# A gated cross-attention and mixture-of-experts layer: expert 0's low weight parts on VectorE, and Silu for the experts' gate

## Chip, core and metric

The kernel runs on one core of a Trainium2 chip. The metric is the device time of one execution in microseconds (us), lower is better. Profile times are us from the start of the span unless ns is written. TensorE does the matmuls (PE in the profile, its weight loads PEld), VectorE is DVE, ScalarE is ACT, GpSimd is POOL, and SyncE (SP) issues most of the transfers.

## What is computed

x is 8 batches of 256 tokens by 512. First a cross attention without softmax is added to x: the score is the sigmoid of a product over the 256 positions, scaled by 1/16. Then a mixture of 16 experts, top 4 per token, is added.

```python
x = x + tanh(g_xattn[0]) * xattn(layernorm(x), ctx, ctx)      # score = sigmoid(Q^T K / 16); out = V score
t = rmsnorm(layernorm(x)) * norm_w
logits = t @ gate_w.T + gate_b
vals, idx = top_k(logits, 4);  gates = softmax(vals)          # scattered to G[token, expert]
h = einsum('mh,eoh->emo', t, w1) + b1
a = minimum(h[..., ::2], 7.0)
b = clip(h[..., 1::2], -7.0, 7.0)
act = a * sigmoid(1.702 * a) * (b + 1.0)
y = einsum('emi,edi->emd', act, w2) + b2
x = x + tanh(g_ffn[0]) * einsum('me,emd->md', G, y)
```

## The kernel before

**Split products.** The large matmuls take their fp32 operands in two parts: a rounded high part (ScalarE writes it, `W1h`, `W2h`, `xTh`, `hTh`, `Kh`, `Qh`), and the low part, which is the value less the high part (`W1l`, `W2l`, `xTl`, `hTl`, `Kl`, `Ql`). Each product is three passes: high by high, low by high, high by low.

**Attention stage** (0 to some 145 us). The engines each run an own list, written out by hand, over the batches b = 0 to 7. TensorE: products of K and Q (`qk`, L397), of scores and V (`av`, L409), turning of the normed tokens of batch b-1 (L417), their logits (L426), and the rank of the tokens within an expert (`rank`, L437). ScalarE: sigmoid of the scores, the scale of the tokens (`scale_t`, L615, which waits for GpSimd's `p_rs1`), high parts of K and Q, the output's base, one weight chunk's high part per batch for b = 0 to 5 (`high`, L639 and L641), and the copy of the turned tokens for the logits (`tTs`, L621). VectorE: choice of the top 4 (`choose`), statistics, `base_scale` (L852, waits for GpSimd's `p_rs1`), `gates` (L884), `ln_bias` (L809), `places` (writes `dst`, L904), then `low_k` and `low_q`, and per half `add_x` (L817, waits for `av`). GpSimd: for each batch two small powers (`x1_scale` L1143, `ln_scale` L1139) and eight scatters of table entries (`put`, L1152, waits for `dst` and the gates of that batch).

**Expert 0's weights** have to be split before the expert stage. Its first weights have four chunks, c = 0 to 3, its second weights two, c = 4 and 5. VectorE does c = 1 in batch 2 and c = 4 and 5 in batches 5 and 6 (L909, L912). GpSimd does c = 0, 2 and 3 in its batches 1, 3 and 4 (L1156). SP may load expert 1's chunk over `W1f` only once expert 0's low part of the chunk is there, so it waits for these too, in its batches 3 to 6.

**Between the stages** the last scatters run, VectorE works out a table of the work units, the placement table is read back, and the first tokens are gathered by GpSimd (L1188).

**Expert stage** (some 176 us to the end). A loop over 24 units; a unit is up to four tiles of 128 tokens of one expert. For each of four blocks i of 128 hidden values, TensorE writes the a half to PSUM bank `PA[i % 2]` and the b half to `PB[i % 2]` (L555, 24 matmuls for each block), and between block 0 and block 1 the second layer of the unit before (L501), which waits for `e_hl`, the last low part of the hidden values. Before block i it waits for `e_lo1` (the low part of the weights) and for `e_af` and `e_bf` (ScalarE has read the banks of two blocks ago). ScalarE, `gate(i)`: `sg` (L721), `av` (L722) and `bw` (L726); also the high parts of the hidden values (L746), of the gathered tokens (L685) and of the next expert's weights (L751, L732), and the scaled output (L703). VectorE, `hidden(i)`: `bv` (L1074), `uu` (L1076), `hv` (L1078), then `low_h` (L1082) and `low_w` (L1087). ScalarE's and VectorE's blocks are tied: `hv` needs `bw`, `hTh` needs `hv`, `hTl` needs `hTh`, and each engine works its list in order. The widths are 256, 384 or 512 tokens.

Of the kernel before, what the change touches and what calls it, by code (L numbers as in the profile page):

```python
# [7 lines left out]
ALU = mybir.AluOpType  # L8
AF = mybir.ActivationFunctionType
F32 = mybir.dt.float32  # L10
# [6 lines left out]
B = 8  # L17
S = 256
H = 512
# [15 lines left out]
ALPHA = 1.702  # L35
SIG7 = float(1.0 / (1.0 + np.exp(-ALPHA * LIMIT)))
TE = CAP // 128
# [43 lines left out]
def build(nc, x, ctx, ctxT, gx, gf, nw, gw, gb, wts, bias, b1t, cst, out):  # L81
    with ExitStack() as es:
# [35 lines left out]
        av_at = sb.place[0]  # L118
        av_ = [sb(f"av{i}", [128, H]) for i in range(2)]
        bw = [sb(f"bw{i}", [128, H]) for i in range(2)]  # L120
        bv = [sb(f"bv{i}", [128, H]) for i in range(2)]
        sg = [sb(f"sg{i}", [128, H]) for i in range(2)]
        hv = [sb(f"hv{i}", [128, H]) for i in range(2)]
        uu = sb("uu", [128, H])
        C = sb("C", [128, C_N])
# [116 lines left out]

        e_hi1, e_lo1, e_lop, e_hi2, e_lo2, e_b1, e_bc, e_go = (sem(n) for n in ("e_hi1", "e_lo1", "e_lop", "e_hi2", "e_lo2", "e_b1", "e_bc", "e_go"))
        e_tx, e_xh, e_xl = sem("e_tx"), sem("e_xh"), sem("e_xl")
        e_l1a, e_l1b, e_af, e_bf, e_sg, e_cc, e_uu, e_h, e_hh, e_hl = (sem(n) for n in ("e_l1a", "e_l1b", "e_af", "e_bf", "e_sg", "e_cc", "e_uu", "e_h", "e_hh", "e_hl"))
        e_l2, e_yb, e_ys, e_gv, e_gp, e_ga = sem("e_l2"), sem("e_yb"), sem("e_ys"), sem("e_gv"), sem("e_gp"), sem("e_ga")
# [20 lines left out]
        def sp(e):  # L267
# [61 lines left out]
            for b in range(B):  # L329
# [15 lines left out]
                if 3 <= b < 3 + N1:  # L345
                    e.wait_ge(*((e_lop, 1), (e_lo1, N1), (e_lop, 2), (e_lop, 3))[b - 3])
                    load_w(1, b - 3)
# [31 lines left out]
        def pe(e):  # L379
# [142 lines left out]
            for j in range(4):  # L522
                e.wait_ge(d_first[j], 16)
                turn_x(j, 1, ys, P0[j])
                run_idle(1 if j < 3 else 3)
            e.wait_ge(e_lop, 3)
            with e.Fori(0, n) as u:
# [58 lines left out]
        def act(e):  # L586
# [96 lines left out]
            def high_x(j, r, par, P_=PX):  # L683
                e.wait_ge(e_tx, r)
                e.copy(xTh[:, par, :, 128 * j:128 * j + 128], P_[:].rearrange("p (c t) -> p c t", c=4)).then_inc(e_xh, 1)  # L685

            e.wait_ge(d_base, 16 * B)
            e.wait_ge(e_b1, 2)
# [19 lines left out]
            with e.Fori(0, n) as u:  # L708
# [9 lines left out]
                def gate(i, w, between=None):  # L718
                    now_ = e.snap(u * 4 + (i + 1))
                    e.wait_ge(e_l1a, now_)  # L720
                    e.activation(sg[i % 2][:, 0:w], PA[i % 2][:, 0:w], AF.Sigmoid, scale=ALPHA, bias=bcur[:, 2, i:i + 1]).then_inc(e_sg, 1)  # L721
                    e.activation(av_[i % 2][:, 0:w], PA[i % 2][:, 0:w], AF.Identity, bias=bcur[:, 0, i:i + 1]).then_inc(e_af, 1)  # L722
                    if between:
                        between()
                    e.wait_ge(e_l1b, now_)
                    e.activation(bw[i % 2][:, 0:w], PB[i % 2][:, 0:w], AF.Identity, bias=bcur[:, 1, i:i + 1]).then_inc(e_bf, 1)  # L726

# [66 lines left out]
        def dve(e):  # L794
# [111 lines left out]
            def low(c):  # L906
                if c < N1:
                    e.wait_ge(e_hi1, c + 1)
                    e.tensor_tensor(W1l[:, c, :, :], W1f[:, c, :, :], W1h[:, c, :, :].bitcast(F32), ALU.subtract).then_inc(e_lo1, N1)  # L909
                else:  # L910
                    e.wait_ge(e_hi2, c - N1 + 1)
                    e.tensor_tensor(W2l[:, 0, half2(c)], W2f[:, 0, half2(c)], W2h[:, 0, half2(c)].bitcast(F32), ALU.subtract).then_inc(e_lo2, 1)  # L912
# [12 lines left out]
            for b in range(B):  # L925
# [16 lines left out]
                if b == 0:  # L942
                    e.wait_ge(d_c, 16)
                    e.wait_ge(v_mm0, 1)
                    e.tensor_scalar(SUb[:], C[:, C_SU:C_SU + 128], float(TE), None, op0=ALU.mult).then_inc(v_su, 1)
                if b in (2, 5, 6):
                    low((1, 4, 5)[(2, 5, 6).index(b)])
                if b + 1 < B:
# [13 lines left out]
            e.wait_ge(d_b1, 16)  # L962
            e.tensor_scalar(b1s[:, :, 1, :], b1s[:, :, 1, :], 1.0, None, op0=ALU.add).then_inc(e_b1, 1)
            e.tensor_scalar(b1s[:, :, 2, :], b1s[:, :, 0, :], ALPHA, None, op0=ALU.mult).then_inc(e_b1, 1)
# [84 lines left out]
            with e.Fori(0, n) as u:  # L1049
# [21 lines left out]
                def hidden(i, w):  # L1071
                    now_ = e.snap(u * 4 + (i + 1))
                    e.wait_ge(e_bf, e.snap(u * 4 + (i + 3)))
                    e.tensor_scalar(bv[i % 2][:, 0:w], bw[i % 2][:, 0:w], 1 - LIMIT, 1 + LIMIT, op0=ALU.max, op1=ALU.min).then_inc(e_cc, 1)  # L1074
                    e.wait_ge(e_cc, now_)
                    e.scalar_tensor_tensor(uu[:, 0:w], av_[i % 2][:, 0:w], LIMIT, bv[i % 2][:, 0:w], ALU.min, ALU.mult).then_inc(e_uu, 1)  # L1076
                    e.wait_ge(e_uu, now_)
                    e.scalar_tensor_tensor(hv[i % 2][:, 0:w], sg[i % 2][:, 0:w], SIG7, uu[:, 0:w], ALU.min, ALU.mult).then_inc(e_h, 1)  # L1078

# [53 lines left out]
        def pool(e):  # L1133
# [19 lines left out]

            def low(c):
                e.wait_ge(e_hi1, c + 1)
                e.tensor_tensor(W1l[:, c, :, :], W1f[:, c, :, :], W1h[:, c, :, :].bitcast(F32), ALU.subtract).then_inc(e_lop, 1)  # L1156

            ln_scale(0)
            for b in range(B):
                if b >= 1:  # L1160
                    x1_scale(b - 1)
                if b + 1 < B:
                    ln_scale(b + 1)
                if b in (1, 3, 4):
                    low((0, 2, 3)[(1, 3, 4).index(b)])
                if b >= 2:
# [137 lines left out]
```

## Time and profile before

| | |
|---|---|
| median of 3 runs | 834.03 us (833.62 to 834.31) |
| the profiled execution | 835.31 us, its span 833.5 us |
| granted TensorE clock, mean | 0.969 |
| TensorE busy | 772.3 us, 93% of the span |
| weight loads on TensorE | 657.1 us, 79% |
| VectorE busy | 519.8 us, 62% |
| ScalarE busy | 459.4 us, 55% |
| GpSimd busy | 314.8 us, 38% |

The profile is one execution. Its lines give the start and the duration of an instruction, and in brackets the idle time of the engine before it and what ended that. "issue" is idle time in which the engine waited for nothing that the profile shows. A matmul's end is modelled. The granted clock is given as a share of full speed.

### The profile page before, as it was taken

The page shows a single profiled execution, that of the slowest core. Times are in us where ns is not written, and L with a number is a line of the kernel's source. Part 1 is how long each engine was busy: PE and PEld are TensorE (multiplying, and loading weights), DVE is VectorE, ACT ScalarE, POOL GpSimd, SP SyncE. Part 2 cuts the span into 40 slices and gives each one's busy share as a digit, 9 for nine tenths or more (in the row PEclk, how much of TensorE's full clock was granted, in tenths as well). Part 3 has the DMA queues.
Part 4 walks back from the last instruction along what each step waited for, and adds up shares of the span by engine and source line. Part 5 has one row for each costly group of instructions (what it writes and reads, how often), then busy time and mean ns, then how long its engine had stood idle before and what let it go on. Part 6 is the DMA issues. An engine that isn't in the chain of part 4 may idle for free.

```text
span 833.5 us, 16730 instructions
## 1 busy us (share of the span) xinstructions
PE 772.3 (93%) x4067; PEld 657.1 (79%) x4068; DVE 519.8 (62%) x1020; ACT 459.4 (55%) x785; POOL 314.8 (38%) x290
## 2 busy tenths in 40 slices
PE   9999897189999999999999999999999989999984
PEld 3665675179889889888888988898998978898873
DVE  3898885437667664667568656657556575756541
ACT  4666654036557555656557656547456565646530
POOL 0267776632342413431522343324343333325212
PEclk9999898589999999999999999999999999999997
DMA  7756563145747645555847854537455454544312
GB/s 286 229 186 202 194 177 115 14 131 154 161 120 211 156 132 152 120 148 160 201 96 206 212 122 114 148 97 176 126 108 139 100 161 111 152 122 75 38 26 39
DMA packets 107768, 117.02 MB, mean 140 GB/s; under 512 B 11808, under 2 KB 77344, under 8 KB 107744
## 3 DMA queue, kind: packets, MB, share of 16 engines
q1 hardware_dynamic: 88896, 77.32, 30.0%
q0 software_dynamic: 18848, 39.40, 23.9%
q8 instruction: 12, 0.20, 0.1%
q14 instruction: 12, 0.10, 0.0%
HBM read 88.06 MB, written 28.94 MB: 140 GB/s over the span
## 4 chain that ended last, share of the span: by engine, by line
PE 78%; DVE 8%; issue 5%; ACT 3%; POOL 3%; DMA 1%; ACTq 0%; another core or an unknown queue 0%; DVEq 0%; POOLq 0%
PE ps L555 39%; PE ps L501 25%; PE ps L409 4%; PE ps L480 3%; PE ps L397 3%; POOL tab L1152 2%; PE ps L426 2%; DVE uu L1076 1%; DVE W1l L1087 1%; PE ps L392 1%; DVE hv L1078 1%; DMA xg<-rows,srcI 1%; PE ps L417 1%; ACT hTh L746 1%; DVE bv L1074 1%
## 5 line engine op out<-in xcount | busy, mean ns | idle before, releaser
L555 PE MATMUL ps<-xTh,W1h 128*128 x768 | 257.9, 336 | 12.7 <-issue 10.7
L555 PE MATMUL ps<-xTh,W1l 128*128 x768 | 250.4, 326 | 0.0
L555 PE MATMUL ps<-xTl,W1h 128*128 x768 | 250.3, 326 | 0.0
L1235 POOL DMA_INDIRECT out<-ys,dgI x75 | 118.5, 1579 | 311.9 <-ACT ys L703 289.5
L555 PEld LDWEIGHTS ps<-xTh,W1h 128*128 128x128 f32 x768 | 144.6, 188 | 23.1 <-issue 18.4
L555 PEld LDWEIGHTS ps<-xTh,W1l 128*128 128x128 f32 x768 | 144.6, 188 | 5.2
L555 PEld LDWEIGHTS ps<-xTl,W1h 128*128 128x128 f32 x768 | 144.8, 189 | 4.8
L501 PE MATMUL ps<-W2h,hTh 128*128 x300 | 118.8, 396 | 7.7 <-DVE hTl L1082 7.7
L703 ACT ACTIVATE ys<-ps,dgI 128x512 f32<-128x512 f32 x75 | 51.7, 689 | 122.0 <-DVE ps L1047 119.9
L501 PE MATMUL ps<-W2l,hTh 128*128 x300 | 118.1, 394 | 0.0
L501 PE MATMUL ps<-W2h,hTl 128*128 x300 | 117.9, 393 | 0.0
L1022 DVE TENSOR_TENSOR xTl<-ps,xTh 128x512 f32 (+1 forms) x75 | 51.5, 690 | 98.0 <-ACT xTh L685 96.7
L1178 POOL DMA_INDIRECT xg<-rows,srcI x71 | 82.2, 1157 | 39.0 <-issue 38.0
L746 ACT CAST hTh<-hv 128x384 fp32r<-128x384 f32 (+2 forms) x96 | 50.8, 529 | 67.7 <-DVE hv L1078 64.5
L1047 DVE TENSOR_TENSOR ps<-ps,b2s 128x512 f32<-128x512 f32 x75 | 52.3, 697 | 56.1 <-PE ps L501 53.8
L1152 POOL DMA_INDIRECT tab<-C,dst x64 | 70.5, 1102 | 33.3 <-issue 17.4
L726 ACT ACTIVATE bw<-ps,bcur 128x384 f32<-128x384 f32 (+2 forms) x96 | 57.6, 600 | 39.5 <-PE ps L555 34.0
L1082 DVE TENSOR_TENSOR hTl<-hv,hTh 128x384 fp32r<-128x384 f32 (+2 forms) x96 | 55.2, 575 | 36.5 <-ACT hTh L746 30.2
L1074 DVE TENSOR_SCALAR bv<-bw 128x384 f32<-128x384 f32 (+2 forms) x96 | 36.3, 378 | 63.2 <-ACT bw L726 55.4
L501 PEld LDWEIGHTS ps<-W2h,hTh 128*128 128x128 f32 x300 | 57.0, 190 | 20.7 <-issue 9.3
L1087 DVE TENSOR_TENSOR W1l<-W1f,W1h 128x1024 fp32r<-128x1024 f32 x60 | 73.1, 1219 | 0.0
L721 ACT ACTIVATE sg<-ps,bcur 128x384 f32<-128x384 f32 (+2 forms) x96 | 57.1, 594 | 17.6 <-ACT bcur L762 9.4
(148 smaller groups left out, 1086.0 us busy)
## 6 DMA issues: line engine op xcount, KB each, us to landing
W1f<-in_wts SPq DMA_DIRECT2D x64, 512.0 KB
W2f<-in_wts SPq DMA_DIRECT2D x32, 512.0 KB
X<-in_x SPq DMA_DIRECT2D x8, 512.0 KB
Kt<-in_ctx SPq DMA_DIRECT2D x8, 512.0 KB
Vt<-in_ctxT SPq DMA_DIRECT2D x8, 512.0 KB
rows<-tt SPq DMA_DIRECT2D x8, 512.0 KB
out<-base SPq DMA_DIRECT2D x8, 512.0 KB
b2s<-in_bias SPq DMA_DIRECT2D x16, 256.0 KB
```

The source lines that it names most:

```text
L501: m = e.matmul(PY[j][:], (hTh, hTl)[hl][:, c, 128 * j:128 * j + 128], (W2h, W2l)[wl][:, bass.ds(slot, 1), H * c:H * c + H], start=(t == 0) ...
L555: m = e.matmul(P_[i % 2][:, 0:32 * w], (W1h, W1l)[wl][:, i, 2 * k + h, :], (xTh, xTl)[xl][:, bass.ds(par, 1), k, 0:32 * w], start=(t == 0) ...
L703: e.activation(ys[j][:], PY[j][:], AF.Copy, scale=dgI[:, j, 1:2]).then_inc(e_ys, 1)
L721: e.activation(sg[i % 2][:, 0:w], PA[i % 2][:, 0:w], AF.Sigmoid, scale=ALPHA, bias=bcur[:, 2, i:i + 1]).then_inc(e_sg, 1)
L726: e.activation(bw[i % 2][:, 0:w], PB[i % 2][:, 0:w], AF.Identity, bias=bcur[:, 1, i:i + 1]).then_inc(e_bf, 1)
L746: e.copy(hTh[:, i, 0:w], hv[i % 2][:, 0:w]).then_inc(e_hh, 1)
L1047: e.tensor_tensor(PY[j][:], PY[j][:], b2s[:, bass.ds(side, 1), :].rearrange("p o h -> p (o h)"), ALU.add).then_inc(e_yb, 1)
L1082: e.tensor_tensor(hTl[:, i, 0:w], hv[i % 2][:, 0:w], hTh[:, i, 0:w].bitcast(F32), ALU.subtract).then_inc(e_hl, 1)
L1087: e.tensor_tensor(W1l[:, i, :, :], W1f[:, i, :, :], W1h[:, i, :, :].bitcast(F32), ALU.subtract).then_inc(e_lo1, 1)
L1152: e.indirect_dma_start(tab, bass.IndirectOffsetOnAxis(dst[:, b, q:q + 1], axis=0), pay[:, 2 * b + q // K, q % K, :], None).then_inc(d_put, 16)
L1178: e.indirect_dma_start(xg[j][:], None, rows, bass.IndirectOffsetOnAxis(srcI[:, j, 0:1].bitcast(I32), axis=0)).then_inc(d_g[j], 16)
L1235: e.indirect_dma_start(out, bass.IndirectOffsetOnAxis(dgI[:, j, 0:1].bitcast(I32), axis=0), ys[j][:], None, compute_op=ALU.add).then_inc(d ...
```

## The change

1. Expert 0's low parts `low(0)` to `low(3)` are all written by VectorE, in batches 1 to 4, one in each, behind `places` and ahead of `low_k`. `low(4)` and `low(5)` go to batch 7, at the same place. GpSimd's three are gone, and with them the semaphore `e_lop`; SP waits for `e_lo1` alone, TensorE's wait for `e_lop` ahead of the loop is gone.
2. In the expert stage ScalarE applies Silu to ALPHA * (a half) + bias in place of the sigmoid, and the copy `av` is gone; `e_af` is now raised by the Silu. ALPHA * a * sigmoid(ALPHA * a) is what comes out, so `bw` is scaled by 1/ALPHA, `b1s` and the limits of `bv` likewise. Since Silu grows with its argument above 0, the limit 7 of a becomes the limit TOP_GATE = 7 ALPHA sigmoid(7 ALPHA) of the Silu, in the product `hv`; `uu` is gone.
3. A Silu on two columns is placed behind the last gate sigmoid, ahead of ScalarE's waits for the expert stage.
4. The place of `av_` stays reserved, as the keys' high parts of the attention stage lie there; `uu`'s 2 KB are given back.

```diff
-SIG7 = float(1.0 / (1.0 + np.exp(-ALPHA * LIMIT)))
+TOP_GATE = float(ALPHA * LIMIT / (1.0 + np.exp(-ALPHA * LIMIT)))
...
 def sp(e):
                 if 3 <= b < 3 + N1:
-                    e.wait_ge(*((e_lop, 1), (e_lo1, N1), (e_lop, 2), (e_lop, 3))[b - 3])
+                    e.wait_ge(e_lo1, b - 2)
                     load_w(1, b - 3)
...
 def pe(e):
-            e.wait_ge(e_lop, 3)
             with e.Fori(0, n) as u:
...
 def act(e):
+            e.activation(warm[:], mh[:, 0:2], AF.Silu)
             e.wait_ge(d_base, 16 * B)
...
                     e.wait_ge(e_l1a, now_)
-                    e.activation(sg[i % 2][:, 0:w], PA[i % 2][:, 0:w], AF.Sigmoid, scale=ALPHA, bias=bcur[:, 2, i:i + 1]).then_inc(e_sg, 1)
-                    e.activation(av_[i % 2][:, 0:w], PA[i % 2][:, 0:w], AF.Identity, bias=bcur[:, 0, i:i + 1]).then_inc(e_af, 1)
+                    e.activation(sg[i % 2][:, 0:w], PA[i % 2][:, 0:w], AF.Silu, scale=ALPHA, bias=bcur[:, 2, i:i + 1]).then_inc(e_af, 1)
...
-                    e.activation(bw[i % 2][:, 0:w], PB[i % 2][:, 0:w], AF.Identity, bias=bcur[:, 1, i:i + 1]).then_inc(e_bf, 1)
+                    e.activation(bw[i % 2][:, 0:w], PB[i % 2][:, 0:w], AF.Identity, scale=1.0 / ALPHA, bias=bcur[:, 1, i:i + 1]).then_inc(e_bf, 1)
...
 def dve(e):
                 if c < N1:
                     e.wait_ge(e_hi1, c + 1)
-                    e.tensor_tensor(W1l[:, c, :, :], W1f[:, c, :, :], W1h[:, c, :, :].bitcast(F32), ALU.subtract).then_inc(e_lo1, N1)
+                    e.tensor_tensor(W1l[:, c, :, :], W1f[:, c, :, :], W1h[:, c, :, :].bitcast(F32), ALU.subtract).then_inc(e_lo1, 1)
...
-                if b in (2, 5, 6):
-                    low((1, 4, 5)[(2, 5, 6).index(b)])
+                if 1 <= b <= N1:
+                    low(b - 1)
+                if b == B - 1:
+                    low(N1)
+                    low(N1 + 1)
                 if b + 1 < B:
                     low_k(b + 1)
...
-            e.tensor_scalar(b1s[:, :, 1, :], b1s[:, :, 1, :], 1.0, None, op0=ALU.add).then_inc(e_b1, 1)
+            e.tensor_scalar(b1s[:, :, 1, :], b1s[:, :, 1, :], 1.0, 1.0 / ALPHA, op0=ALU.add, op1=ALU.mult).then_inc(e_b1, 1)
...
-                    e.tensor_scalar(bv[i % 2][:, 0:w], bw[i % 2][:, 0:w], 1 - LIMIT, 1 + LIMIT, op0=ALU.max, op1=ALU.min).then_inc(e_cc, 1)
+                    e.tensor_scalar(bv[i % 2][:, 0:w], bw[i % 2][:, 0:w], (1 - LIMIT) / ALPHA, (1 + LIMIT) / ALPHA, op0=ALU.max, op1=ALU.min).then_inc(e_cc, 1)
                     e.wait_ge(e_cc, now_)
-                    e.scalar_tensor_tensor(uu[:, 0:w], av_[i % 2][:, 0:w], LIMIT, bv[i % 2][:, 0:w], ALU.min, ALU.mult).then_inc(e_uu, 1)
-                    e.wait_ge(e_uu, now_)
-                    e.scalar_tensor_tensor(hv[i % 2][:, 0:w], sg[i % 2][:, 0:w], SIG7, uu[:, 0:w], ALU.min, ALU.mult).then_inc(e_h, 1)
+                    e.scalar_tensor_tensor(hv[i % 2][:, 0:w], sg[i % 2][:, 0:w], TOP_GATE, bv[i % 2][:, 0:w], ALU.min, ALU.mult).then_inc(e_h, 1)
...
 def pool(e):
-            def low(c):
-                e.wait_ge(e_hi1, c + 1)
-                e.tensor_tensor(W1l[:, c, :, :], W1f[:, c, :, :], W1h[:, c, :, :].bitcast(F32), ALU.subtract).then_inc(e_lop, 1)
-
...
-                if b in (1, 3, 4):
-                    low((0, 2, 3)[(1, 3, 4).index(b)])
```

## Rows read from the trace of the kernel before

**Rows 1.** Order in time, TensorE: start, us, engine, line, operation, count [idle before].
```profile
37.81 0.47 PE L397 MATMUL ps<-Kh,Qh 128*128 128x512 f32 x1
...
52.99 0.47 PE L397 MATMUL ps<-Kh,Qh 128*128 128x512 f32 x1
...
85.91 0.79 PE L426 MATMUL ps<-gwT,tTs 128*128 128x16 f32 x3 [2.42 <-ACT tTs L621]
...
121.17 0.47 PE L397 MATMUL ps<-Kh,Qh 128*128 128x512 f32 x1
```

**Rows 2.** By stretch: length, PE, PEld, DVE, ACT, POOL busy, granted clock, DMA share, GB/s.
```profile
83.00:105.00 22.00, 19.58 (x76) 13.66 (x74) 17.79 (x51) 13.65 (x22) 16.14 (x15) 0.84 0.59 192
```

**Rows 3.** Order in time, VectorE, in the attention stage.
```profile
58.93 2.49 DVE L884 TENSOR_TENSOR ex<-s,s 128x8 f32<-128x8 f32 x1
...
61.99 0.15 DVE L809 SCALAR_TENSOR_TENSOR nb<-mv,rs 128x2 f32<-128x2 f32 x1
...
76.13 3.00 DVE L852 TENSOR_SCALAR c<-rs,tg 128x2 f32<-128x2 f32 x1 [1.72 <-POOL rs L1143]
```

**Rows 4.** Order in time, GpSimd: its subtractions for expert 0.
```profile
59.04 2.35 POOL L1156 TENSOR_TENSOR W1l<-W1f,W1h 128x1024 fp32r<-128x1024 f32 x1
...
76.75 2.35 POOL L1156 TENSOR_TENSOR W1l<-W1f,W1h 128x1024 fp32r<-128x1024 f32 x1
```

**Rows 5.** Waits of TensorE, 176 us to the end: us in total, times, longest.
```profile
PE ps L555 <- issue: 10.7, 19, 1.4
PE ps L501 <- DVE hTl L1082: 7.7, 5, 3.7
```

**Rows 6.** Order in time, VectorE: its own low part of expert 0, batch 2.
```profile
45.20 1.22 DVE L909 TENSOR_TENSOR W1l<-W1f,W1h 128x1024 fp32r<-128x1024 f32 x1
```

**Rows 7.** Order in time, GpSimd: powers and scatters.
```profile
57.34 1.05 POOL L1143 TENSOR_TENSOR rs<-ve,mh 128x4 f32<-128x4 f32 x1
...
63.50 1.75 POOL L1152 DMA_INDIRECT tab<-C,dst  x1 [2.11 <-DVE dst L904]
...
75.05 1.04 POOL L1143 TENSOR_TENSOR rs<-ve,mh 128x4 f32<-128x4 f32 x1
...
129.28 1.04 POOL L1152 DMA_INDIRECT tab<-C,dst  x1 [2.71 <-DVE dst L904]
```

**Rows 8.** Order in time, VectorE: the second `add_x` of batch 7.
```profile
134.85 0.75 DVE L817 SCALAR_TENSOR_TENSOR x<-ps,tg,X 128x512 f32<-128x512 f32 x1 [1.83 <-issue]
```

**Rows 9.** Groups by line, shapes together or apart: busy us, mean ns | idle before.
```profile
L722 ACT ACTIVATE av<-ps,bcur 128x384 f32<-128x384 f32 (+2 forms) x96 | 56.6, 589 | 0.0
L1076 DVE SCALAR_TENSOR_TENSOR uu<-av,bv 128x384 f32<-128x384 f32 (+2 forms) x96 | 55.3, 576 | 3.3
...
L721 ACT ACTIVATE sg<-ps,bcur 128x384 f32<-128x384 f32 x52 | 30.2, 580 | 6.3 <-ACT bcur L762 5.4 <-PE ps L555 0.5
```

**Rows 10.** Order in time, TensorE: stops in the expert stage.
```profile
480.48 0.49 PE L501 MATMUL ps<-W2h,hTh 128*128 x1 [0.96 <-DVE hTl L1082]
...
573.84 0.44 PE L555 MATMUL ps<-xTh,W1h 128*128 x1 [1.00 <-ACT av L722]
...
648.73 0.39 PE L555 MATMUL ps<-xTh,W1h 128*128 x1 [0.65 <-issue]
...
673.58 0.49 PE L501 MATMUL ps<-W2h,hTh 128*128 x1 [1.27 <-DVE hTl L1082]
...
810.50 0.79 PE L501 MATMUL ps<-W2h,hTh 128*128 x1 [3.66 <-DVE hTl L1082]
```

**Rows 11.** Chain of work that ended last, 658 to 674 us: shares by line.
```profile
by line: issue 24.2%; DVE W1l L1087 13.9%; ACT hTh L746 10.1%; DVE uu L1076 7.1%; DVE hv L1078 7.1%; ACT W1h L751 6.4%; PE ps L501 4.6%; DVE ps L1047 4.5%; DVE hTl L1082 4.3%; DVE bv L1074 4.0%; ACT sg L721 3.6%; ACT bw L726 3.0%; ACT av L7
```

**Rows 12.** Order in time, ScalarE: last block of the last unit.
```profile
806.96 0.58 ACT L726 ACTIVATE bw<-ps,bcur 128x384 f32<-128x384 f32 x1
```

**Rows 13.** Order in time, ScalarE: its first work for the experts.
```profile
172.23 1.56 ACT L685 CAST xTh<-ps 128x512 fp32r<-128x512 f32 x3 [24.37 <-issue]
```

**Rows 14.** Groups by line, ScalarE: the table load.
```profile
L644 ACT ACT_TABLE_LOAD x1 | 1.3, 1283 | 0.6 <-PEq L1294 0.6
```

More of the change, by code:

```diff
@@ L118, in build @@
         av_at = sb.place[0]
-        av_ = [sb(f"av{i}", [128, H]) for i in range(2)]
+        sb.place[0] += 2 * 4 * H
         bw = [sb(f"bw{i}", [128, H]) for i in range(2)]
@@ L123, in build @@
         hv = [sb(f"hv{i}", [128, H]) for i in range(2)]
-        uu = sb("uu", [128, H])
         C = sb("C", [128, C_N])
@@ L241, in build @@
         v_wa, v_wc, v_rf = sem("v_wa"), sem("v_wc"), sem("v_rf")
-        e_hi1, e_lo1, e_lop, e_hi2, e_lo2, e_b1, e_bc, e_go = (sem(n) for n in ("e_hi1", "e_lo1", "e_lop", "e_hi2", "e_lo2", "e_b1", "e_bc", "e_go"))
+        e_hi1, e_lo1, e_hi2, e_lo2, e_b1, e_bc, e_go = (sem(n) for n in ("e_hi1", "e_lo1", "e_hi2", "e_lo2", "e_b1", "e_bc", "e_go"))
         e_tx, e_xh, e_xl = sem("e_tx"), sem("e_xh"), sem("e_xl")
-        e_l1a, e_l1b, e_af, e_bf, e_sg, e_cc, e_uu, e_h, e_hh, e_hl = (sem(n) for n in ("e_l1a", "e_l1b", "e_af", "e_bf", "e_sg", "e_cc", "e_uu", "e_h", "e_hh", "e_hl"))
+        e_l1a, e_l1b, e_af, e_bf, e_cc, e_h, e_hh, e_hl = (sem(n) for n in ("e_l1a", "e_l1b", "e_af", "e_bf", "e_cc", "e_h", "e_hh", "e_hl"))
         e_l2, e_yb, e_ys, e_gv, e_gp, e_ga = sem("e_l2"), sem("e_yb"), sem("e_ys"), sem("e_gv"), sem("e_gp"), sem("e_ga")
```

## The prediction, made before the changed kernel ran

> **What bounds the kernel now.** I read the waits of TensorE first, then the order in time of TensorE, VectorE, GpSimd and ScalarE in the attention stage, then every stop of TensorE in the expert stage. TensorE is busy 93% of the span, so an edit on another engine is worth only what it takes out of TensorE's stops, or out of the stretch in between in which TensorE stands still and the placement tables are written.
>
> Attention stage, eight batches. Two batches without a disturbance start 15.18 us apart (37.81 and 52.99, [rows 1]). Batch 7 starts at 121.17, five rounds after 37.81: 83.36 us where five undisturbed ones are 75.9. So 7.5 us are lost there, 2.42 of it as one open wait for ScalarE's copy `tTs` at 85.91 [rows 1]; much of the rest follows it, for the granted clock is 0.84 in the stretch from 83 to 105 us [rows 2], a mix of its two levels (2.4 and 1.2 GHz), after TensorE stood for those 2.42 us. Where the late `tTs` comes from is on VectorE: a product of 128x8 takes 2.49 us and a scalar step of 128x2 takes 3.00, where such a step takes 0.15 otherwise [rows 3]. Both end within 0.05 us of GpSimd's `low` (59.04 + 2.35 = 61.39 against 61.42; 76.75 + 2.35 = 79.10 against 79.13) [rows 3, 4]. VectorE was held while GpSimd subtracted. A third pair like them stands at 27.8 us.
>
> Expert stage. TensorE waits 7.7 us in five stops for the low part of the hidden values, `hTl`, and 10.7 us in 19 stops for nothing that the profile names [rows 5].
>
> **Part 1, the low parts of expert 0's first weights: off GpSimd, onto VectorE.** Removed: three GpSimd subtractions of 2.35 us [rows 4], and with them holds on VectorE of 2.49 - 0.2 = 2.3 and 3.00 - 0.2 = 2.8 us (0.2 for a step of their size, 0.15 in the row shown) and 2.2 at 27.8. The first hold costs TensorE nothing, since no stop follows it. Added: `low(0)`, `low(2)`, `low(3)` on VectorE, 1.22 us each [rows 6], in batches 1, 3 and 4; in 3 and 4 VectorE is still ahead by 2.3 - 1.2 = 1.1 and 2.8 - 1.2 = 1.6 us. ScalarE's rounded parts that they wait for are made a batch earlier, so the new waits don't hold. SP's loads of expert 1 wait for these parts at batches 3 to 6 of its own queue, one to three batches after they are written: nothing. If all of the lost time came back, the stage would give 7.5 us.
>
> Not all comes back, for GpSimd's own round is nearly as long as TensorE's. It runs eight scatters, a power for the scales (`rs`), then waits for VectorE's next `dst`. From 57.34 to 75.05 one round took 17.71 us [rows 7]; without the hold of 2.3 that is 15.4, against TensorE's 15.18. And a VectorE subtraction lengthens a scatter that runs beside it: 1.75 us at 63.50 with one beside it, 1.04 at 129.28 with none [rows 7]. Each `low` now stands just ahead of the scatters, in front of the same subtraction of K. Bounds for a `low` there: 0 and 0.7 us; I take 0.3. Rounds of 15.7 in batches 3 and 4 make `rs` late by 0.5 us per batch, which ScalarE has no room to absorb in batches that also carry `high`. I book 0.25, 0.35 and 0.6 us of stops in batches 3, 4 and 5, together 1.2. Phase sum: 7.5 - 1.2 = 6.3 us; bounds 4.5 (scatters at 0.7 each, and 1 us of slow clock kept) and 7.5.
>
> The Trainium skill, SBUF — State Buffer, section Who interferes with whom, says the pair of ports is an exclusive lock, which agrees with the holds above; it also says that a `tensor_tensor` takes only the read side and is inferred not to starve descriptor generation. The 1.75 us scatter speaks against that second half. By the page the 0.3 would be 0 and the gain about 0.6 us more.
>
> **Part 2, the second weights' low parts (`low(4)`, `low(5)`) from batches 5 and 6 to batch 7.** Batches 5 and 6 get 1.2 us of VectorE back, not on TensorE's path. In batch 7 they put 2.4 us ahead of `add_x(7, 0)`. That step runs late by about a microsecond, and the next one waits 1.83 us for TensorE anyway [rows 8], which takes it up: zero. If that cover is gone, up to 1 us. They also stand beside the scatters of batch 5 and delay the last `rs` by up to 0.9 us; the last two sets of scatters run back to back, and their start hangs on TensorE's logits of batch 6, so this costs 0 to 1 us. I take 0.1 of it: phase gain 6.2.
>
> **Part 3, Silu in place of sigmoid, copy and product.** Per hidden block ScalarE loses the copy `av` (589 ns mean, 96 times) and VectorE the product `uu` (576 ns) [rows 9]: 56.6 and 55.3 us of work, almost all beside matmuls. Silu itself has no row. Bounds: a little below the sigmoid on the same operands (580 ns at 128x384, [rows 9]), as the copy is, or up to twice it, which would eat what the copy gives; I take the sigmoid's time, the nearest row. Folding 1/ALPHA into scales and limits adds no instruction. The rest of the blocks' steps stay.
> What it takes out of TensorE's stops, one by one:
> - Stops for `hTl`. The one at 480.48 is 0.96 long and has one product of 0.69 plus 0.03 of hand-over on its way: -0.72. A like one of 0.67 goes: -0.67. At 673.58 (1.27) the chain ahead of it has 7.1% of 16 us in products, 1.1 us [rows 10, 11], and a copy: it goes, -1.27. One like it at 767.81 (1.12) goes too. The last, at 810.50, is 3.66 long: TensorE was done at 806.84, ScalarE began `bw` at 806.96 [rows 10, 12]. From there only the product (0.56 + 0.03) and the 0.12 go: -0.7, and the stop stays at 3.0. Sum 4.5.
> - Three stops at the start of a unit, 573.84 (1.00, for `av`) and two twins of it marked "issue" (0.95, 0.99), where ScalarE frees the PSUM bank late. A bare unit start costs 0.65 (648.73) [rows 10]. They fall to that: -1.0.
> - Small remainders of the same kind (three stops of 0.8): -0.4.
> - The other "issue" stops and those for gathered rows stay.
> Together 5.9 us; bounds 3.5 (only the named `hTl` stops go in part) and 7.5 (the freed chains also shorten waits below 0.2 us that I did not count).
>
> A second table is needed, since the attention stage uses sigmoid. The kernel places a first Silu behind the last gate sigmoid, where ScalarE stands idle for 24.37 us [rows 13]; a load took 1.28 us [rows 14]. Zero, as long as nothing reloads in the loop. The Trainium skill, ScalarE: Activation LUTs, section Table sets: the hidden batching unit, says that cheap functions such as copy and identity are in every set; in this trace one load served sigmoid, tanh, identity and copy, which agrees as far as it goes. The same page gives a switch about 2.7 us with its drain; by it the sum is the same, as that too fits into the 24 us.
>
> **The sum.** 6.2 + 5.9 = 12.1 us. On the profiled execution's own 835.3 us (span 833.5 and 1.8 around it) that makes 823.2; it ran 1.3 above the median of 834.03, which goes to 821.9. I forecast 822.
>
> **Rivals.**
> A. The attention gain is given back. GpSimd's scatters become the bound of that stage (its round is 15.4 to 15.7 against 15.18), or a stop over 2 us remains and the clock falls again. For it: the bare margin. Against: the rounds before 53 us keep 15.18 with the same scatters. Then only part 3 and some 1 to 2 us: 834.0 - 5.9 - 1.5 = 826.6.
> B. The expert gain is absent, as the stops are TensorE's own sequencing ("issue" has more than `hTl`) or Silu is as slow as sigmoid plus copy. Then 6.2 plus at most the products' share of 2: 826 to 828.
> C. More than booked: every lost microsecond of the attention stage (7.5), and the small waits (7.5): 819, below that hardly.
> D. Slower than before: the copies are not served by Silu's table and each block reloads twice. 96 blocks x 2 x 1.28 us [rows 9, 14] = 246 us on ScalarE, each load in the middle of a block, between `sg` and `bw`. It decides as soon as ScalarE's block is longer than TensorE's, which is the case first in the narrow blocks; 52 of the 96 are 384 wide [rows 9]. With two loads less the copy that went, 2.57 - 0.58 = 2.0 us, added to a block whose chain already stops TensorE, I price 1 to 2 us for each of the 52: 50 to 100 us more, so about 900. For it only that the trace shows no Silu; against it the one load that served four functions.
> E. The holds on VectorE were not GpSimd's doing, so the three added subtractions cost and nothing returns: at most 3 x 1.2 - 5.9, still faster, 831. The equal ends speak against it.
>
> **How the numbers follow.** Forecast 0.62, from 819 to 825. A 0.13, B 0.11, C (below 819) 0.07, D 0.03, E 0.04. The range leaves out D, E, the far part of B and the tail of C: 817.5 to 827. A change of 0.2% (1.7 us, about what a measurement of this kernel can tell from none) is passed by all cases but D and a bad form of E: faster 0.94, same 0.02, slower 0.04.
>
> **What would show it.** In the profile after: no GpSimd subtraction, no small VectorE step over 1 us in the first 130 us, batch starts 15.2 to 15.8 apart, batch 7's at about 115, granted clock near 1.00 from 83 to 105, the experts' first matmul near 170.5 instead of 176.69. In the experts: stops for `hTl` about 3.2 us in all, nearly all of it in the last unit, none for `av`; ScalarE some 57 and VectorE some 59 us less busy (55 of products, 7 of holds, less 4 added); two table loads in all, the second before the experts. It is wrong if batch starts stay at 16 or more, if a reload stands in the loop, or if the stops at 573 and 673 keep their length.

## The result, and the profile after

The changed kernel took 825.98 us in the median of four runs (821.62 to 827.25), the kernel before 834.17 beside it (833.62 to 834.64): a ratio of 0.9893, 95% interval 0.9856 to 0.993. In two later sets, on chips 8 and 9 (the first set's chip isn't on record), the same kernel took 821.95 (821.86 to 822.58) and 821.74 us (821.1 to 822.67), ratios 0.9857 [0.9835, 0.9879] and 0.9857 [0.9839, 0.9875]. One of the eight runs of the kernel before beside the first of these sets took 2716.5 us, and no time or ratio here uses it. So it is faster, by 8 us in the first set and by 12 in the later ones. The profiled execution of the first set took 826.44 us, its span 824.5.

The page after, its parts 1 and 2:

```profile
span 824.5 us, 16539 instructions
...
PE 766.4 (93%) x4067; PEld 653.8 (79%) x4068; DVE 463.4 (56%) x927; ACT 417.9 (51%) x691; POOL 304.1 (37%) x287
...
PEclk9999997599999999999999999999999999999997
```

VectorE has 56.4 us less to do than before, ScalarE 41.5, GpSimd 10.7. TensorE, which bounds the kernel, is busy 5.9 us less with the same matmuls.

The attention stage after, in order of time, TensorE: the starts of batches 2, 3, 5 and 7. They answer to [rows 1].

```profile
37.86 0.47 PE L396 MATMUL ps<-Kh,Qh 128*128 128x512 f32 x1
...
53.04 0.47 PE L396 MATMUL ps<-Kh,Qh 128*128 128x512 f32 x1
...
83.83 0.48 PE L396 MATMUL ps<-Kh,Qh 128*128 128x512 f32 x1
...
114.47 0.47 PE L396 MATMUL ps<-Kh,Qh 128*128 128x512 f32 x1
...
119.13 0.50 PE L396 MATMUL ps<-Kh,Qh 128*128 128x512 f32 x1 [1.65 <-ACT Sc L608]
```

Batch 7 starts at 114.47 where it started at 121.17: 6.7 us came back. Five rounds take 76.6 us, against 75.9 for five undisturbed ones. The stop of 2.42 us is gone, and in this trace the slow clock behind it. By stretch (the columns of [rows 2]):

```profile
83.00:105.00 22.00, 21.96 (x101) 15.43 (x101) 19.32 (x73) 13.22 (x24) 16.15 (x16) 1.00 0.68 216
```

In the same 22 us TensorE now issues 101 matmuls at a granted clock of 1.00, and did 76 at 0.84 [rows 2]. VectorE's held steps, which answer to [rows 3], in order of time:

```profile
59.00 0.17 DVE L882 TENSOR_TENSOR ex<-s,s 128x8 f32<-128x8 f32 x1
...
59.74 0.16 DVE L807 SCALAR_TENSOR_TENSOR nb<-mv,rs 128x2 f32<-128x2 f32 x1
...
73.76 0.23 DVE L850 TENSOR_SCALAR c<-rs,tg 128x2 f32<-128x2 f32 x1 [0.37 <-POOL rs L1142]
```

0.17 and 0.23 us, where they took 2.49 and 3.00.

But of the 6.7 us only 3.7 arrive at the experts, whose first matmul stands at 172.97 (before 176.69). The stop of 1.65 us at 119.13, above, is one place where the rest went: ScalarE began that sigmoid late. Another is VectorE's start on the logits of batch 6, again in order of time:

```profile
118.48 1.09 ACT L608 ACTIVATE Sc<-ps 128x512 f32<-128x512 f32 x2 [6.67 <-PE ps L396]
...
134.35 0.19 DVE L855 TENSOR_TENSOR Lg<-ps,gbb 128x32 f32<-128x32 f32 x1 [1.49 <-remote]
```

The expert stage takes 651.5 us after its first matmul, 656.8 before. TensorE's waits there, 176 us to the end (us in total, times, longest), answering to [rows 5]:

```profile
PE ps L553 <- issue: 5.5, 11, 1.1
PE ps L500 <- DVE hTl L1081: 3.2, 2, 3.0
PE ps L553 <- DVE W1l L1086: 2.9, 3, 1.0
PE ps L553 <- ACT bw L724: 2.1, 3, 0.8
```

The stops on `hTl` fell from 7.7 us in five to 3.2 in two. Those that the profile calls "issue" only seem to have halved. Part of them carry another name now, W1l or bw, at the same places and lengths (below), and the window from 176 us leaves out the stop of the first unit after the change (0.99 at 172.97), which it counts before (1.36 at 176.69). With that one in, the stops ahead of the first layer's matmuls, under any name, were 12.5 us in 21 before and are 11.5 in 18.

The single lines behind my three claims on ScalarE. First, the load of Silu's table, with the idle time behind it; then Silu and bw by form (busy us, mean ns), to be held against 580 and 588 ns of the sigmoid and the bw of the same width before:

```profile
143.24 1.28 ACT L685 ACT_TABLE_LOAD   x1
...
167.79 1.22 ACT L683 CAST xTh<-ps 128x512 fp32r<-128x512 f32 x2 [23.05 <-issue]
...
L724 ACT ACTIVATE bw<-ps,bcur 128x384 f32<-128x384 f32 x52 | 30.3, 583 | 35.5 <-PE ps L553 28.2 <-issue 6.0 <-remote 1.2
L720 ACT ACTIVATE sg<-ps,bcur 128x384 f32<-128x384 f32 x52 | 30.3, 582 | 8.5 <-ACT bcur L760 5.4 <-PE ps L553 1.8 <-issue 0.8
```

### The profile page after: what moved, and what is told of

Its sections match the earlier page's. It is cut to its first block, busy times and chain, and to the rows that moved or that the text cites. A ratio compares the mean times of both kernels' runs of the same rounds, so it can differ in the third digit from the quotient of the medians.

```text
span 824.5 us, 16539 instructions
## 1 busy us (share of the span) xinstructions
PE 766.4 (93%) x4067; PEld 653.8 (79%) x4068; DVE 463.4 (56%) x927; ACT 417.9 (51%) x691; POOL 304.1 (37%) x287
## 4 chain that ended last, share of the span: by engine, by line
PE 82%; issue 7%; DVE 3%; DMA 3%; ACT 2%; POOL 1%; ACTq 0%; DVEq 0%; POOLq 0%; another core or an unknown queue 0%; SPq 0%
PE ps L553 40%; PE ps L500 24%; PE ps L408 7%; PE ps L396 5%; PE ps L479 4%; DMA xg<-rows,srcI 2%; PE ps L425 1%; DVE W1l L1086 1%; PE ps L391 1%; PE ps L416 1%; POOL out L1228 1%; DVE bv L1075 0%; ACT bw L724 0%; DMA ys<-rows,src 0%; DVE ps L1048 0%
## 5 line engine op out<-in xcount | busy, mean ns | idle before, releaser
L1171 POOL DMA_INDIRECT xg<-rows,srcI x71 | 75.9, 1069 | 39.2 <-issue 37.9
L500 PEld LDWEIGHTS ps<-W2l,hTh 128*128 128x128 f32 x300 | 57.0, 190 | 12.1
```

Source lines behind the costliest of these rows:

```text
L500: m = e.matmul(PY[j][:], (hTh, hTl)[hl][:, c, 128 * j:128 * j + 128], (W2h, W2l)[wl][:, bass.ds(slot, 1), H * c:H * c + H], start=(t == 0) ...
L1171: e.indirect_dma_start(xg[j][:], None, rows, bass.IndirectOffsetOnAxis(srcI[:, j, 0:1].bitcast(I32), axis=0)).then_inc(d_g[j], 16)
```

## The experiments

The parts are numbered as in the prediction: 1 and 2 are the low parts, 3 is Silu. The theory that I set out to test: the attention stage gains because GpSimd's subtractions no longer hold VectorE (theory H), the experts gain because VectorE's chain to `hTl` is one product shorter (theory V), the two add up, and the 3 us lost between 114 and 173 us belong to an execution and not to the change (theory W). Rivals are named with each run. Unless it says otherwise, a kernel is the changed one with the edit shown, in shortened code; times are medians, and the kernel before ran beside the sets at 833.35 to 833.84.

**again and again_2: the changed kernel, unchanged**

> The changed kernel once more, nothing edited. Its four runs lay between 821.6 and 827.3 us, while the kernel before keeps within 1 us. Theory W (the 3 us that the profiled execution lost between batch 7 and the experts are stops that differ from one execution to the next): the times scatter again over some 5 us, and in this trace the 1.65 us stop of TensorE at 119 us (for the scores' sigmoid) or the 1.49 us stop of VectorE at 134 us has another length or another place. Theory F (they are fixed costs of the new order): both stand where they stood, within 0.3 us, and the times scatter for another reason.

Measured: 821.95 us; batch 7 at 114.55, the logits of batch 6 at 130.90, the experts' first matmul at 169.7, the expert stage 650.5. No stop of TensorE at batch 7's start. The times did not scatter again over 5 us, as theory W had expected. Once more, on another chip:

> The changed kernel once more, unchanged. Its first runs gave 821.6 to 827.3 us and the set after them 821.9 to 822.6. Theory W (a 3 us loss between batch 6 and the experts' first matmul comes and goes from one execution to another, and is no part of the change): the times lie near 822 or near 826 and nowhere else, and the profiled run shows either both stops (TensorE at batch 7's start on a late sigmoid of ScalarE, 1.7 us, and VectorE's Lg late by 1.5 us) with the experts' first matmul near 173, or neither with it near 170. Rival (the first result, 826, is the kernel's true time and the set at 822 had a chip that favours it): 826 again with both stops.

Measured: 821.74 us (five runs, 821.1 to 822.67), the first matmul at 169.9, the expert stage 651.1, again neither stop. From the trace of again, in order of time, the same two steps of ScalarE and VectorE:

```profile
116.22 0.60 ACT L608 ACTIVATE Sc<-ps 128x512 f32<-128x512 f32 x1 [4.34 <-PE ps L396]
...
130.90 0.18 DVE L855 TENSOR_TENSOR Lg<-ps,gbb 128x32 f32<-128x32 f32 x1
```

In again ScalarE takes the sigmoid up at 116.22; in the first profile it took it up at 118.48. Two of three profiles of the changed kernel lack the 3 us, and by their times one of the first four runs (821.62) and all nine later ones do. So the 3 us are not in every execution of it. That leaves the first set's chip as a possible cause, beside chance. What made ScalarE late isn't settled. In the first trace a packet of the instruction queue moved from 118.34 to 118.83 us, beside the start of the late sigmoid. It isn't the cause by itself: again and again_2 have such a packet at 118.48 and 118.33, without a stop, and the late sigmoid began before its packet had ended. That stays open.

**silu_only: the kernel before with part 3 alone**

```diff
-e.activation(sg, PA, AF.Sigmoid, scale=ALPHA, bias=bcur[:, 2])     # then av, a copy
+e.activation(sg, PA, AF.Silu, scale=ALPHA, bias=bcur[:, 2])
-uu = min(av, LIMIT) * bv;  hv = min(sg, SIG7) * uu
+hv = min(sg, TOP_GATE) * bv
```

> Part 3 alone: Silu in place of sigmoid, copy and product; the low parts stay on GpSimd and VectorE as before. Theory of the prediction: the experts' stage gives 5.3 us (what the changed kernel's trace shows from the experts' first matmul to the end), the attention stage stays as before with batch 7 at 121.2; time 828 to 829. Rival (the gain of the experts is an effect of the earlier start, not of Silu): time 833 to 834.

Measured: 826.95 us (825.49 to 830.32), ratio 0.992 [0.9892, 0.9947]. The holds and the stops of the attention stage are those of before: c takes 3.01 us, TensorE stops for 2.42 us at 86.03. Yet batch 7 starts at 119.8, 1.4 us earlier than before and than I had expected, and the time is 1 to 2 us under my 828 to 829. The clock behind the same stop fell less, to 0.92 against 0.84 [rows 2]:

```profile
83.00:105.00 22.00, 19.57 (x86) 13.46 (x85) 18.84 (x54) 13.89 (x23) 16.28 (x15) 0.92 0.64 201
```

By this comparison some 1.4 of the 6.7 us that batch 7 won hang on the one execution that the profile before shows. The expert stage takes 650.4 us, 6.4 less than before, and the waits on `hTl` are 3.2 us in two.

**lows_only: parts 1 and 2 alone, with sigmoid, copy and product kept**

> Parts 1 and 2 alone: expert 0's low parts all on VectorE, sigmoid, copy and product kept. Theory of the prediction: batch 7 starts at 114.5 instead of 121.2, the experts stage keeps its 656.8 us; time 827.5 if all 6.7 us arrive, 830.5 if the 3 us are lost again as in the changed kernel's trace. Rival A (GpSimd's scatters take over as the bound): batch starts over 15.5 apart and 832 or more.

Measured: 828.33 us (827.32 to 829.45), ratio 0.9927 [0.9903, 0.9951]. Batch 7 starts at 114.4, the first matmul stands at 170.0 (−6.7), the expert stage takes 657.7 with 7.7 us of `hTl` stops in five, as before. The two ratios multiply to 0.9848, and the whole change has 0.9857: within the intervals, the parts don't interfere.

**second_lows_early: part 2 undone (`low(4)`, `low(5)` back in batches 5 and 6)**

```diff
-if b == B - 1: low(N1); low(N1 + 1)
+if b in (5, 6): low(b - 1)
```

> The changed kernel, but the second weights' low parts back in batches 5 and 6 as before, in place of batch 7. Theory of the prediction: they cost nothing at either place, so the time is that of the changed kernel within 1 us. Rival: the two of them in batch 7 (2.35 us at 121.95) delay the last batch and with it the scatters' start; then this one is 1.5 to 3 us faster than the changed kernel, and VectorE's choice of batch 6 starts at 133 or earlier instead of 134.35.

Measured: 821.67 us (819.71 to 821.89), ratio 0.9844 [0.9819, 0.987], against 821.95 for the changed kernel on that chip. The scatters of batch 6 and the experts' first matmul stand where they did. GpSimd, in order of time, the first scatters of batches 5 and 6, first with part 2 undone:

```profile
122.57 1.03 POOL L1150 DMA_INDIRECT tab<-C,dst  x1 [2.71 <-DVE dst L902]
...
135.47 1.09 POOL L1150 DMA_INDIRECT tab<-C,dst  x1 [1.71 <-DVE dst L902]
```

The same two in again, the changed kernel:

```profile
121.39 1.75 POOL L1151 DMA_INDIRECT tab<-C,dst  x1 [2.71 <-DVE dst L902]
...
135.53 1.09 POOL L1151 DMA_INDIRECT tab<-C,dst  x1 [1.61 <-DVE dst L902]
```

With part 2 undone the scatters of batch 5 begin 1.2 us later, as a `low` ahead of each of the two sets before them made these longer (11.42 and 11.58 us, against 10.75 and 10.70 in the changed kernel's first profile). They take 10.13 us then, where they take 11.41 in again beside the two moved `low`, and so end at the same time (132.69 and 132.81). The cost of the `low` has moved from one place of GpSimd's queue to another, and part 2 is worth nothing. This version can't be told from the changed kernel.

**copy_back: ScalarE's copy without the product**

```diff
 e.activation(sg[i % 2], PA[i % 2], AF.Silu, ...)
+e.activation(av_[i % 2], PA[i % 2], AF.Identity, ...)   # nobody reads it; e_af comes from here
```

> The changed kernel with ScalarE's copy of the gate put back behind the Silu (96 copies of 0.6 us, into tiles that nobody reads; the TensorE waits for them before it overwrites the bank, as it did before). Theory V (the experts' gain of 6 us is that of VectorE's chain, one product shorter): within 1 us of the changed kernel, about 822.3; the hTl stops of the middle of the stage stay away. Rival S (the gain is ScalarE's, which has 57 us less to do and so makes hTh and the next weights' high parts earlier): 4 to 6 us slower, 826 to 828, with hTl stops back at 0.5 to 1.1 us each. If both share it: about 825. The three stops of 0.96 us at unit starts, which my prediction put down to this copy, should grow by nothing if it was wrong in that (the run with the copy removed kept them).

Measured: 821.98 us (821.52 to 822.81), ratio 0.9862 [0.9841, 0.9884]; the kernel without the copy, again_2 on the same chip, 821.74. ScalarE is busy 463.6 us again, the expert stage takes 650.7, the last stop on `hTl` is 2.98 long. The copy was free, as far as the spread tells.

**product_back: VectorE's product without the copy**

```diff
 bv = max/min(bw)
+av_[i % 2] = min(sg, LIMIT) * bv     # nobody reads it
+e.wait_ge(e_uu, now_)
 hv = min(sg, TOP_GATE) * bv
```

> The changed kernel with a second product on VectorE put back into each hidden step (96 of about 0.58 us, result unread, but hv waits for it as it did before). Theory V: 4 to 6 us slower, 826 to 828, the last stop on hTl back from 3.0 to 3.6 us and the ones of 0.7 to 1.3 us back. Rival S: within 1 us of the changed kernel, about 822.3.

Measured: 827.02 us (826.85 to 827.18), ratio 0.9922 [0.9901, 0.9943]: 5.3 us slower than again_2. TensorE's waits from 165 us on:

```profile
PE ps L553 <- issue: 9.0, 15, 1.2
PE ps L500 <- DVE hTl L1083: 7.5, 5, 3.6
```

The last of these stops, in order of time:

```profile
803.04 0.69 PE L500 MATMUL ps<-W2h,hTh 128*128 x1 [3.58 <-DVE hTl L1083]
```

With one product of 576 ns back in each block, four more stops on `hTl` are back (0.66, 0.95, 1.23 and 1.12 us, before 0.67, 0.96, 1.27 and 1.12), and the last goes from 2.98 to 3.58. Theory V holds; rival S, which gave the gain to ScalarE's relief, is out. The product added here also makes VectorE 53 us busier than in again_2 (515.8 against 462.8), so this run alone doesn't part the length of the chain from VectorE's load; the length of the last stop does speak for the chain, 0.60 longer by a product of 0.56 at this width.

**pool_sub_scratch: GpSimd's subtraction without its data**

```diff
 # GpSimd; W2f[:, 1, 0:1024] is cleared once at the start; SP's loads of W2f in its batches 6 and 7 wait for the last of these
+if b in (3, 4):
+    e.tensor_tensor(W2f[:, 1, 1024:2048], W2f[:, 1, 0:1024], W2f[:, 1, 0:1024], ALU.subtract)
```

> The changed kernel with two GpSimd subtractions of 128x1024 put where the kernel before had its own in batches 3 and 4, but of scratch that nobody waits for (plus a memset at the start): all of expert 0's low parts stay on VectorE, and no semaphore of the changed kernel hangs on them. Theory H (an operation of GpSimd holds VectorE's small steps for as long as it runs): VectorE's ex and c steps in batches 3 and 4 take 2 to 3 us again, the batch starts behind them lie 0.8 and 4 us later, TensorE stops for about 2.4 us at 86 and its clock falls between 83 and 105; 4 to 6 us slower than the changed kernel, 826 to 828. Rival E (the holds come from waiting for W1l, or from what the subtraction's own data are): batches 15.2 to 15.8 apart and no more than 0.5 us slower.

Measured: 825.83 us (824.59 to 828.15), ratio 0.9907 [0.988, 0.9935]: 4.1 us slower than again_2. That is 0.2 us under my 826 to 828. Two of its runs took 824.6 us, the others 827.0 (the traced one) and 828.2. In order of time, VectorE's `ex` and GpSimd's scratch operation, batch 3 and batch 4:

```profile
58.87 2.03 DVE L883 TENSOR_TENSOR ex<-s,s 128x8 f32<-128x8 f32 x1
58.98 1.89 POOL L1164 TENSOR_TENSOR W2f<-W2f 128x1024 f32<-128x1024 f32 x1
60.93 0.16 DVE L885 TENSOR_REDUCE zz<-ex 128x2 f32<-128x8 f32 x1
...
75.96 2.04 DVE L883 TENSOR_TENSOR ex<-s,s 128x8 f32<-128x8 f32 x1
76.09 1.88 POOL L1164 TENSOR_TENSOR W2f<-W2f 128x1024 f32<-128x1024 f32 x1
```

`ex` ends at 60.90, GpSimd at 60.87; at 78.00 and 77.97 again. No engine waits for this operation (SP's loads of that tile do, batches later) and its data touch nothing that VectorE reads, so the hold comes from the two engines at work side by side: theory H holds, rival E (a matter of `W1l` or of the waits) is out. Nor is it GpSimd's own list that got too long: after each operation it stood idle for 2.1 us, waiting for VectorE's `dst`, as it did in the kernel before [rows 7]. Both holds fell on `ex`. The one on `c` before, which began 0.6 us ahead of GpSimd's subtraction (76.13 against 76.75), isn't repeated here, and its first 0.6 us stay unexplained. What follows is the story of before, in small: the starts of batches 4, 5, 6 and 7 are 0.6, 2.3, 3.3 and 5.0 us later than in again_2. My expectation had a stop of 2.4 us at 86; there was one of 0.67 at 67.24 and one of 0.93 at 100.85, and the granted clock was low about both: 0.88 from 65 to 70 us and 0.80 from 100 to 105, and from 70 to 75 us by stretch:

```profile
70.00:75.00 5.00, 5.00 (x20) 3.82 (x20) 4.65 (x22) 1.39 (x4) 4.06 (x5) 0.78 0.94 304
```

**pool_copy_scratch: a copy, with one input, in its place**

```diff
-e.tensor_tensor(W2f[:, 1, 1024:2048], W2f[:, 1, 0:1024], W2f[:, 1, 0:1024], ALU.subtract)
+e.tensor_copy(W2f[:, 1, 1024:2048], W2f[:, 1, 0:1024])
```

> The changed kernel with a GpSimd copy (one input) of 128x1024 of scratch in batches 3 and 4, where the run with the scratch subtraction (two inputs) had that. Theory L (any GpSimd operation over 128x1024 of the SBUF holds VectorE): ex takes as long as the copy runs, about 1 to 2 us, batch 5 starts 0.5 to 2.3 us late, 823 to 826. Rival T (only a two-input operation of GpSimd holds it): ex 0.16 us, batches 15.2 to 15.8 apart, within 0.5 us of the changed kernel, about 822.

Measured: 823.88 us (823.06 to 824.78), ratio 0.9877 [0.985, 0.9904]. Order in time:

```profile
59.01 1.16 DVE L883 TENSOR_TENSOR ex<-s,s 128x8 f32<-128x8 f32 x1
59.11 1.03 POOL L1164 COPY W2f<-W2f 128x1024 f32<-128x1024 f32 x1
```

The copy holds `ex` too, for its own length (59.11 + 1.03 = 60.14; `ex` ends at 60.17), and so again in batch 4 (1.15 us). Batch 4 starts on time, batches 5 and 7 are 1.0 and 3.3 us late against again_2. Theory L holds: one input is enough on GpSimd's side.

**pool_sub_pieces: the subtraction in four pieces of 128x256**

> The changed kernel with the same scratch subtractions as before on GpSimd, each cut into four of 128x256 (about 0.5 us each). Theory P (each operation of GpSimd holds VectorE for its own length and lets it in between two): three or four of VectorE's small steps take 0.4 to 0.6 us in place of one that takes 2.0; the sum of the holds is then about the same, batch 5 starts about 2.3 us late again, 825 to 826. Rival Q (VectorE gets in early enough that its chain of small steps is hardly late): holds of under 0.6 us in all, batches 15.2 to 15.8 apart, about 822.

Measured: 826.45 us (825.96 to 826.81), ratio 0.9908 [0.9882, 0.9934]. Order in time:

```profile
58.98 2.46 DVE L883 TENSOR_TENSOR ex<-s,s 128x8 f32<-128x8 f32 x1
59.10 2.31 POOL L1165 TENSOR_TENSOR W2f<-W2f 128x256 f32<-128x256 f32 x4
61.47 0.16 DVE L885 TENSOR_REDUCE zz<-ex 128x2 f32<-128x8 f32 x1
```

The time is 0.45 us above the 825 to 826 of theory P, and still both theories missed: VectorE doesn't get in between two pieces. The one small step waits for all four, in batch 4 too (2.47 us), and since they take 2.31 us together where the whole took 1.89, cutting made it no better (TensorE stops of 1.10 at 67.8, 1.94 at 85.3 and 0.93 at 101.8). Behind none of these stops did the granted clock fall: it is 1.00 in each stretch of 5 us from 60 to 130.

## Why the prediction was right or wrong, point by point

The forecast of 822.0 lies within the range of the first set and 4 us below its median; the two later sets stand at 821.95 and 821.74. The first median alone, 825.98, lies outside the 819 to 825 of the forecast's own case and fits rivals A (826.6) and B (826 to 828) as well. It is the traces and the runs with one part alone that decide for the forecast's mechanism. The sum of 12.1 us met the later sets (11.6 to 11.9 us under the kernel before beside them), but not each term did.

- **The holds were GpSimd's.** Right, and shown: scratch operations bring them back, and the batches late with them. The slow clock of [rows 2] followed the stop that they caused, and 0.84 became 1.00. How much such a stop costs in clock isn't fixed, though: behind the same stop of 2.42 us silu_only had 0.92, and pool_sub_pieces 1.00 behind one of 1.94.
- **Booked back, 1.2 us in the attention stage.** Somewhat too much. The 7.5 us lost became 0.7: batch 7 starts 6.7 earlier, the sum had 6.3; but part of the 7.5 was that execution's clock (silu_only, above). No stop over 0.4 us is left in batches 3 to 5, where I booked three; what remains is batches of 15.2 to 15.5 us.
- **A VectorE subtraction lengthens a scatter beside it; 0.3 us for a `low` there.** The reason was half right. What counts is not what runs beside a scatter but what runs as it begins. Order in time, after the change, a first scatter that begins 0.37 us into a `low`, and one that begins 0.10 us ahead of the subtraction of K:

```profile
76.14 1.22 DVE L907 TENSOR_TENSOR W1l<-W1f,W1h 128x1024 fp32r<-128x1024 f32 x1
76.51 1.76 POOL L1151 DMA_INDIRECT tab<-C,dst  x1 [2.10 <-DVE dst L902]
...
91.96 1.03 POOL L1151 DMA_INDIRECT tab<-C,dst  x1 [2.10 <-DVE dst L902]
92.06 1.22 DVE L819 TENSOR_TENSOR Kl<-Kt,Kh 128x1024 fp32r<-128x1024 f32 x1 [0.39 <-ACT Kh L597]
```

  The first ends at 78.27, 0.91 us after the `low` (77.36). In before, after and second_lows_early nearly every scatter that began inside such a subtraction ended 0.83 to 0.91 us behind its end, and the undisturbed ones take 0.95 to 0.98. VectorE's subtraction takes 1.22 us in all cases. So a `low` just ahead of the scatters costs their set 0.7 to 0.9 us (second_lows_early against the changed kernel), and my 0.3 was too low for it. It cost nothing against the kernel before in batches 1 and 2, whose sets took 11.5 us there and take 11.4 and 11.6: before, the first scatter began 0.38 us into the subtraction of K and took 1.75 too [rows 7]. That the term came out near nothing was luck.
- **The Trainium skill, SBUF — State Buffer, section Who interferes with whom.** The exclusive lock agrees with the holds, with two things that the traces add: a held step begins some 0.1 us ahead of GpSimd's operation (58.87 and 58.98), and it isn't let in between four of them. By the section's other half, the inference that a `tensor_tensor` doesn't starve descriptor generation, the term was 0 and not 0.3. The rows above speak against that half, as far as a scatter shows descriptor generation: whether its descriptors wait or its read of `dst`, no run here parts.
- **Part 2 at 0.1 us.** Right: second_lows_early is 0.3 us away, within the spread.
- **The experts' first matmul near 170.5.** 169.6 to 170.0 in the profiles of six kernels and sets, 172.97 in the first. The 3 us were not in the prediction, in no rival either; an execution can have them.
- **The stops for `hTl`, 4.5 us.** Right in sum (7.7 to 3.2) and one by one: three gone, 0.96 down to 0.23, the last 3.66 to 2.98, forecast 3.0. product_back gives them all back. The copy, to which I gave 0.12 of the last one, has no share that copy_back can show.
- **Three stops at unit starts, 1.0 us.** Wrong. They were 0.95, 1.00 and 0.99 and are 0.97, 0.96 and 0.97, so the sign of being wrong that the prediction gave for the stop at 573 did come. In order of time, two of them after the change:

```profile
568.07 0.43 PE L553 MATMUL ps<-xTh,W1h 128*128 x1 [0.96 <-DVE W1l L1086]
...
707.05 0.43 PE L553 MATMUL ps<-xTh,W1h 128*128 x1 [0.97 <-DVE W1l L1086]
```

  The step that failed is the reading of [rows 10]: the row at 573.84 names `av`, and I took the name for the cause, and the 0.65 of another unit start for the bare price. With `av` gone the row names `W1l`, the next thing that happened to end just then, and the length is the same; copy_back has 1.02, 0.98 and 1.01. What the trace does show is a pattern. Of the 23 units that follow another, the ten that follow a unit with matmuls 0.12 to 0.13 us apart all start with a stop of 0.6 to 1.0 us, of the other 13 one (0.6); those of 0.95 to 1.0 are just the three where the next unit's matmuls are 0.17 us apart. It is the same in before, after and the experiments looked at. TensorE's own work between two units, which long matmuls cover, would explain it. I didn't test that.
- **Small remainders, 0.4 us.** Wrong for the same reason: 0.77, 0.81 and 0.80 became 0.81, 0.81 and 0.79.
- **Why the sum of part 3 still fits.** It gained 5.3 to 6.4 us for 5.9 forecast. Stops over 0.4 us in the expert stage fell by 3.7 us (17.5 to 13.8); the rest, 1.6 us in after and 2.8 in again, is time in which TensorE was at its matmuls, which took 625.4 us before and 623.8 or 622.6 after. So 1.4 us of stops that I had booked never came, and shorter matmuls that I had not booked stood in for them. product_back (623.8) doesn't say whether they come from the missing stops, as again_2 without them has 624.0. That stays open.
- **Silu at the sigmoid's price.** Right: 582 against 580 ns at 384 columns, 692 against 689 at 512, 477 against 476 at 256. Two table loads, the second at 143.24 in the idle time, none in the loop. The Trainium skill, ScalarE: Activation LUTs, section Table sets: the hidden batching unit, has the cheap functions in every set; one load now served Silu, identity and copy for 96 blocks, which agrees. Rival D had no ground.
- **Busy times.** VectorE −56.4 for −59 forecast; ScalarE −41.5 for −57. I had added up durations. Activations that follow each other overlap: at 501.88 and 502.25 before, each 0.47 long, they start 0.37 apart. copy_back has 45.8 us more of busy time than again_2 for 96 copies of 592 ns, or 0.48 each.
- **The rivals.** A (attention gain given back) is refuted by lows_only, B (no gain in the experts) by silu_only, E by pool_sub_scratch. C (819) wasn't reached. The figure for E, 834.0 + 3.6 - 5.9, is 831.7 and not 831.

## What to carry to other kernels

Before moving a long elementwise operation to GpSimd to relieve VectorE, look at what VectorE does beside it: here each subtraction held one step of 0.2 us for 2 to 3 us, and cutting it in pieces didn't help. A releaser's name on a short stop is the last event before it and not its cause; when the same stop stands at every start of a like kind, it belongs to the loop. And of two instructions removed per block, only the one on the chain that TensorE waited for paid here: the product was worth 5.3 us, the copy on ScalarE 0.2, which the spread doesn't tell from nothing.

## What the runs showed of the hardware that I had not expected

- Four GpSimd operations of 128x256 in a row held a VectorE step of 128x8 through all of them, 2.46 us, without letting it in between; together they took 2.31 us, one of 128x1024 took 1.89.
- A scatter of GpSimd that begins inside a VectorE subtraction of 128x1024 ends 0.83 to 0.91 us after it (1.75 us in all for one that begins 0.37 us in); one that begins 0.10 us ahead of it takes 1.03.
- A GpSimd copy with one input holds VectorE as a subtraction with two does: 1.16 us for a copy of 1.03.
- A subtraction of 128x1024 took GpSimd 1.89 us on scratch and 2.35 where it read `W1f` and `W1h` [rows 4]; the scratch one read the same data twice and wrote plain fp32. Which of the two makes the difference isn't shown.
- A stop of TensorE of 0.67 us at 67.24 was followed by a granted clock of 0.78 from 70 to 75 us, while in the kernel before a stop of 1.13 us at 67.8 was followed by 1.00 in those 5 us. In pool_sub_pieces stops of 1.10, 1.94 and 0.93 us were followed by no fall, and the same stop of 2.42 us by 0.84 in one kernel and 0.92 in another over 22 us.
